# A hand-timed scan schedule: every slot constant moved, and one state merge out of four dropped

## The reference

```
L0: gated linear recurrence, y = Wout(silu(ga) * gb * scan(f, z)) + x
    top-1 of 4 experts, silu(x Wg) * (x Wu), Wd
L1: xz = W_in x ; xc = silu(conv4(x) + b) ; dt, B, C = W_x xc
    delta = softplus(W_dt dt + b_dt) ; A = -exp(A_log)
    state[n] = exp(delta * A[n]) * state[n] + (delta * xc) * B[n]     n = 0..15
    y = sum_n state[n] * C[n] + D * xc ; y = y * silu(z) ; out = W_out y + b_out
    out = out * silu(bw x) + x                (binarised weight)
```

## Time and profile before

| | |
|---|---|
| median of 3 runs | 1398.58 us (1398.46 to 1400.58) |
| the profiled execution | 1398.58 us, span of its instructions 1396.8 us |
| granted TensorE clock, mean | 0.997 |
| state-space part, first scan to last | 605.7 to 1379.3 us |
| a chunk in its middle, scan to scan | 97.5 us |
| accumulating DMAs that merge states | 31, of 1026 KB each |

### The profile page before, as it was taken

The page is one execution under the profiler, slowest core; times in us unless marked ns, Lnnn a source line. Parts: engine busy times, 40 slices in busy tenths (PEclk is TensorE's granted clock), DMA queues, the critical chain, the costliest instruction groups (busy, mean ns, idle before and its releaser), DMA issues.

```text
span 1396.8 us, 23943 instructions
## 1 busy us (share of the span) xinstructions
PE 1331.7 (95%) x8796; PEld 1064.4 (76%) x8796; DVE 1008.4 (72%) x1358; ACT 875.5 (63%) x1459; POOL 854.0 (61%) x482
## 2 busy tenths in 40 slices
PE   7999999999999999989899999999999999998998
PEld 4444559999999988967667877777778678677777
DVE  7755543323322343578998999999999989989897
ACT  3211121111111132559999999999999999999983
POOL 3222211222222222348989989989989899899894
PEclk9999999999999999999999999999999999999999
DMA  9931126677667755415453553735636554634542
GB/s 298 397 112 60 53 74 232 246 260 266 251 245 254 276 204 211 162 49 90 110 103 79 99 116 77 138 92 97 133 66 125 107 99 93 136 78 104 124 102 65
DMA packets 113187, 205.46 MB, mean 147 GB/s; under 512 B 57647, under 2 KB 84399, under 8 KB 108214
## 3 DMA queue, kind: packets, MB, share of 16 engines
q1 hardware_dynamic: 93814, 146.75, 31.9%
q0 software_dynamic: 19264, 57.26, 19.8%
HBM read 141.78 MB, written 31.00 MB: 124 GB/s over the span
## 4 chain that ended last, share of the span: by engine, by line
PE 54%; ACT 31%; DVE 9%; issue 3%; POOL 2%; DMA 1%; SPq 0%; DVEq 0%; ACTq 0%; POOLq 0%
PE bank L1666 18%; ACT dA L947 13%; ACT dbuT L936 10%; PE bank L1611 9%; PE bank L1679 9%; DVE hst L1509 4%; PE bank L1840 4%; PE bank L1720 2%; PE bank L1848 2%; PE bank L1712 2%; PE bank L1731 2%; PE bank L1860 2%; PE bank L1641 2%; ACT xpad L878 1%; ACT xpad L874 1%
## 5 line engine op out<-in xcount | busy, mean ns | idle before, releaser
L1509 DVE TENSOR_TENSOR_SCAN hst<-dA,carry,bank 128x512 f32<-128x512 f32 x512 | 628.8, 1267 | 37.3 <-PE bank L1840 29.9
L740 POOL TENSOR_TENSOR hst<-hst,c_bc 128x2048 f32<-128x2048 f32 x127 | 550.1, 4425 | 42.1 <-DVE hst L1509 31.3
L947 ACT ACTIVATE dA<-delta,negA 128x512 f32<-128x512 f32 x512 | 354.5, 713 | 1.0 <-DVE hst L1509 0.9
L1840 PE MATMUL bank<-ident,dbuT 128*128 128x128 f32 x2048 | 310.8, 276 | 27.4 <-DVE hst L1509 23.6
L1840 PEld LDWEIGHTS bank<-ident,dbuT 128*128 128x128 f32 x2048 | 239.5, 141 | 127.2 <-DVE hst L1509 57.1
L936 ACT ACTIVATE dbuT<-duT,bT 128x512 f32<-128x512 f32 x382 | 271.6, 712 | 0.3 <-PE bank L1840 0.3
L1666 PEld LDWEIGHTS bank<-f_sb,w_gu 128*128 128x128 f32 x2240 | 256.0, 192 | 4.7 <-issue 2.1
L1666 PE MATMUL bank<-f_sb,w_gu 128*128 128x128 f32 x2240 | 256.9, 275 | 0.7 <-ACT f_sb L804 0.7
L1860 PE MATMUL bank<-ident,hst 128*128 128x128 f32 x1520 | 209.7, 273 | 1.8 <-DMA hst<-hst 1.7
L670 POOL TENSOR_TENSOR x_sb<-x_sb,neg_half 128x1 f32<-128x1 f32 x35 | 22.7, 648 | 271.3 <-DVE x_sb L1290 271.3
L1860 PEld LDWEIGHTS bank<-ident,hst 128*128 128x128 f32 x1520 | 174.2, 141 | 2.6 <-DMA hst<-hst 2.6
(11 more groups left out here) (220 smaller groups left out, 1663.9 us busy)
## 6 DMA issues: line engine op xcount, KB each, us to landing
w_gu<-in_w_gu SPq DMA_DIRECT2D x35, 2048.0 KB
c_bc<-c_rows SPq DMA_DIRECT2D x64, 512.0 KB, 4.4
hst<-hst POOLq DMA_DIRECT2D x31, 1026.0 KB, 9.1
sorted_x<-sg_a SPq DMA_DIRECT2D x12, 387.0 KB, 11.7
x_sb<-sorted_x SPq DMA_DIRECT2D x35, 129.0 KB
x_sb<-in_x SPq DMA_DIRECT2D x8, 512.0 KB, 7.8
w_d<-in_w_d SPq DMA_DIRECT2D x1, 4096.0 KB, 19.9
x_mix<-x_sb SPq DMA_DIRECT2D x1, 4096.0 KB, 30.6
```

What stands on the lines that cost most here:

```text
L740: pool.tensor_tensor(h[:, :, :CH], h[:, :, 1:], c, ALU.mult).then_inc(hc_ready, 1)
L947: act.activation(dA[:, at % DA_BUFS, :], delta[q % B][:, d, :], ACT.Exp, scale=negA[:, d, n:n + 1]).then_inc(dA_ready, 1)
L1509: v.tensor_tensor_scan(h[:, d, 1:], dA[:, at % DA_BUFS, :], bank[4 + u % 2][:], carry1[q % B][:, n, d:d + 1], ALU.mult, ALU.add).then_inc( ...
L1840: ins = pe.transpose(bank[4 + u % 2][:, i * P:(i + 1) * P], dbuT[(DS * q + n) % DBU_BUFS][:, i, d * P:(d + 1) * P], ident[:])
```

## The change

It only replaces tables. Nearly every placement moves by one to six units. Besides that the pair `5: 4` leaves `MERGES` and `LAST_MERGES`: states 4 and 5 are now both added by TensorE, and since (4, d) has no entry in `SUM_AT` it falls to slots 31 to 34. POOL makes states 5, 6, 8 and 11 of dbuT instead of 4, 6, 7 and 9. `DL0` moves to bank A and `XN0` to bank B, so that all four `DL` products share bank A. The tables of the last chunk (`LAST_...`) stay, but it uses `SUM_AT`, `PE_Z`, `PE_G`, `PE_SKIP` and the new merges too.

```diff
-POOL_SPREADS = (4, 6, 7, 9)
+POOL_SPREADS = (5, 6, 8, 11)
-PE_X = (-3, -1, 2, 3, 4, 5, 8, 9)
-PE_G = (11, 12, 15, 16)
-PE_DT = (21, 24, 25, 27)
-PE_DL = (29, 32, 37, 44)
-PE_BC = 31
-PE_BT = 47
-PE_DUT = (49, 51, 52, 56)
-PE_Z = (9, 9, 10, 11, 11, 12, 14, 14)
-PE_XN = (53, 55)
-PE_YF = (21, 30, 34, 36)
-PE_OUT = (40, 42, 43, 45, 46, 47, 49, 51)
-PE_SKIP = (17, 18, 18, 18)
-ACT_X = (1, 5, 10, 11)
+PE_X = (-4, -1, 0, 3, 5, 8, 9, 10)
+PE_G = (12, 14, 15, 16)
+PE_DT = (22, 23, 24, 26)
+PE_DL = (28, 34, 36, 41)
+PE_BC = 32
+PE_BT = 48
+PE_DUT = (51, 53, 54, 55)
+PE_Z = (9, 10, 10, 11, 11, 12, 13, 14)
+PE_XN = (55, 57)
+PE_YF = (21, 32, 35, 37)
+PE_OUT = (39, 40, 42, 44, 46, 47, 49, 51)
+PE_SKIP = (17, 18, 19, 19)
+ACT_X = (3, 6, 11, 16)
-ACT_SOFT = (35, 39, 41, 47)
-ACT_DUT = (51, 54, 55, 59)
-ACT_YF = (24, 36, 39, 40)
-DVE_CONV = (1, 3, 4, 5, 6, 7, 9, 10, 11, 12, 13, 14)
-DVE_GATE = (8, 9, 10, 12)
+ACT_SOFT = (34, 38, 43, 44)
+ACT_DUT = (54, 55, 57, 59)
+ACT_YF = (29, 37, 38, 40)
+DVE_CONV = (2, 3, 4, 5, 6, 8, 9, 10, 11, 12, 13, 14)
+DVE_GATE = (8, 9, 10, 11)
 DVE_DT = 28
-DVE_DELTA = (31, 36, 43, 47)
-DVE_BC = 32
-DVE_BT = 48
+DVE_DELTA = (31, 36, 41, 47)
+DVE_BC = 35
+DVE_BT = 50
-DVE_RESULT = (46, 52)
-DVE_XN = (54, 57)
-POOL_DU = (7, 9, 11, 12)
+DVE_RESULT = (45, 54)
+DVE_XN = (57, 59)
+POOL_DU = (6, 9, 9, 10)
-MERGES = {1: 0, 5: 4, 9: 8, 13: 12}
-LAST_MERGES = {1: 0, 5: 4, 9: 8}
+MERGES = {1: 0, 9: 8, 13: 12}
+LAST_MERGES = {1: 0, 9: 8}
...
-          (15, 1): 6, (15, 2): 8, (15, 3): 3, ... (5, 0): 38, (5, 1): 38, (5, 2): 35,
-          (5, 3): 41, (6, 0): 34, (6, 1): 35, (6, 2): 39, (6, 3): 35, (7, 0): 42, (7, 1): 46, (7, 2): 43, (7, 3): 48,
+          (15, 1): 8, (15, 2): 7, (15, 3): 7, ... (5, 0): 36, (5, 1): 40, (5, 2): 35,
+          (5, 3): 40, (6, 0): 42, (6, 1): 40, (6, 2): 43, (6, 3): 42, (7, 0): 44, (7, 1): 46, (7, 2): 45, (7, 3): 48,
...
-BANK_OF = {..., "DL0": 1, "DL1": 0, "DL2": 0, "DL3": 0, ... "XN0": 0, "XN1": 1, ...}
+BANK_OF = {..., "DL0": 0, "DL1": 0, "DL2": 0, "DL3": 0, ... "XN0": 1, "XN1": 1, ...}
```

More of the change, by code:

```diff
@@ L89 @@
 ACT_BC = None
-DVE_RESULT = (46, 52)
-DVE_XN = (54, 57)
-POOL_DU = (7, 9, 11, 12)
+DVE_RESULT = (45, 54)
+DVE_XN = (57, 59)
+POOL_DU = (6, 9, 9, 10)
 POOL_RES = 13
-MERGES = {1: 0, 5: 4, 9: 8, 13: 12}
-LAST_MERGES = {1: 0, 5: 4, 9: 8}
-SUM_AT = {(13, 0): 6, (13, 1): 4, (13, 2): 8, (13, 3): 6, (14, 0): 2, (14, 1): 2, (14, 2): 1, (14, 3): 2, (15, 0): 4,
[5 rows of a table removed]
-BANK_OF = {"X0": 0, "X1": 1, "X2": 0, "X3": 1, "G0": 0, "G1": 1, "DT": 0, "DL0": 1, "DL1": 0, "DL2": 0, "DL3": 0,
-           "BT": 0, "DUT0": 0, "DUT1": 0, "DUT2": 1, "DUT3": 0, "XN0": 0, "XN1": 1, "YF0": 1, "YF1": 0, "YF2": 1,
+MERGES = {1: 0, 9: 8, 13: 12}
+LAST_MERGES = {1: 0, 9: 8}
+SUM_AT = {(13, 0): 4, (13, 1): 4, (13, 2): 6, (13, 3): 6, (14, 0): 4, (14, 1): 3, (14, 2): 3, (14, 3): 5, (15, 0): 4,
[5 rows of a table added]
+BANK_OF = {"X0": 0, "X1": 1, "X2": 0, "X3": 1, "G0": 0, "G1": 1, "DT": 0, "DL0": 0, "DL1": 0, "DL2": 0, "DL3": 0,
+           "BT": 0, "DUT0": 0, "DUT1": 0, "DUT2": 1, "DUT3": 0, "XN0": 1, "XN1": 1, "YF0": 1, "YF1": 0, "YF2": 1,
            "YF3": 1, "BC": 1, "OUT0": 1, "OUT1": 1}
```

## The result

The changed kernel takes 1421.51 us (median of 4 runs, 1421.28 to 1421.61), beside 1399.43 us for the kernel before in the same sittings (4 runs, 1398.46 to 1400.58): a ratio of 1.0157, 95% interval 1.014 to 1.0175. It is slower, as forecast, by 22 us (1.6%) where 11 were forecast, and lies above the range of 1390 to 1418.

A forecast was written before the change was run, and what follows sets the result against it. No engine stood out; the chain ran DVE, TensorE to the skip term, then ACT, with TensorE to take ACT's place. Six middle chunks x 1.9 = 11.4, less 0.5 for chunk 0, on 1398.58 gave 1409 us, range 1390 to 1418.

The forecast's parts named there:

- ACT's stretch: From the skip term on, ACT nearly alone on the chain for 54 us; to get 2.45 us shorter per chunk.
- xc at t = 35.95: ACT's step after the skip term: predicted to start at t = 36.0, 0.7 us later in the chunk.
- no wait of BC: BC, now in the other bank, no longer waits for `DL0`: a stall of 1.71 us of TensorE gone.
- `DL0` and `DL2` wait 0.30 and 0.81: Slots 28 and 36: `DL0` waits 0.4 us for DVE's copy of dt, `DL2` 0.8 for `make_delta` 1.
- the idle in front of slot 39: Slots 37 and 38 are light and TensorE can't run ahead of the scans: 0.7 us idle.
- 22.65 - 21.8: TensorE's time from slot 8 to the skip term's end: 22.65 us to slot 19, before 21.8 to slot 18.
- the walk: Slot-by-slot estimate of a middle chunk from single-chunk prices, reaching scan 23 at 40.7 us and scan 48 at 77.9.
- the chunk is 77.9 + 21.5 = 99.4: +1.9 us: Middle chunk: scan 48 at 77.9 us, then 21.5 to the next chunk's first scan; 1.9 us longer than before.
- Chunk 0 ... ACT's saving counts: -0.5: Chunk 0: TensorE has room without output projection, so ACT's saving counts; -0.5 us, between -1.7 and +0.7.
- ACT sets the pace: Rival, chance 0.20: TensorE's light slots absorb the additions, each of 7 chunks gains 1.75 us; 1386 us.
- A wash: Rival, chance 0.12: BC's removed wait pays for the four additions, ACT's saving for the later skip term; 1398.6 us.
- More bank waits: Rival, chance 0.10: ACT's lead is too small and `DL3` in slot 41 waits 1.8 us per chunk; 1422 us.

The follow-up runs named there:

- The `DL` run: Kernel after with `DL0` and `DL2` claimed one slot later, PE_DL = (29, 34, 37, 41): 1412.94 us.
- POOL's tables alone: Kernel before with only POOL_SPREADS and POOL_DU as changed: 1402.90 us.
- the run with slots 40 to 44 spread out: Kernel after with two additions of state 5 moved from slot 40, to slots 38 and 39: 1421.22 us.
- the kernel with three mendings: Kernel after with two `DL` claims one slot later, two additions moved out of slot 40 and the merge of state 4 put back: 1409.73 us.
- mid: Kernel before with only the tables of slots 21 to 47 as changed, merge of state 4 kept: 1431.23 us.
- the BC edit with POOL's tables: Kernel before with the BC edit and the change's POOL_SPREADS and POOL_DU: 1405.35 us.
- the BC edit: Kernel before with B and C's product two slots later, DVE_BC at 35 and two turned y one slot later: 1409.72 us.
- the skip-term run: The kernel with three mendings, with the skip term back in its old slots (17, 18, 18, 18): 1416.83 us.
- ACT's copy moved: Kernel before with the BC edit and ACT's copy of the second turned y in slot 34 instead of 36: 1418.11 us.

## Why the prediction was half right

**Right.** The direction and its reason: TensorE's work and its bank waits take the place of ACT's stretch. By its own signs: xc at t = 35.95; an idle before it below 1 us; no wait of BC; `DL0` and `DL2` wait 0.30 and 0.81 (0.4 and 0.8 were written), and the idle in front of slot 39 is 0.59 (0.7 was written); DVE's longest idle behind scan 23 before scan 44, ended by L1840 (over the whole chunk the 0.94 before scan 21 and the 1.80 before scan 23 are longer, which was not written); TensorE on the chain behind xc, though only to t = 70.

Part of the hit at xc is luck: 22.65 - 21.8 and the 0.25 in slot 9 make 1.1, not 0.7, and the 0.7 came of setting the walk's 35.8 against the measured 35.1, where the same walk gives 34.7 for the kernel before.

The rule of the Trainium skill to rotate banks ("Perfetto Trace Analysis", Matmuls) agrees with the trace in one place, not two: `DL2` waits 0.81 us for its bank, while `DL0`'s 0.30, which the prediction counted to the rule, is for its operand. The `DL` run shows what such waits cost, by claiming later; no run puts one of these products into the other bank by itself. The rule on the same page of the Trainium skill to look for the engine with the highest occupancy, and to judge TensorE by its weight loads ("Identifying the Most-Contended Engine"), misleads here: these fill 74.0 of 96 us, yet 1.74 us more of TensorE's work cost 1.05 us. Whether less work for ACT, the busiest by that rule, would pay, no run shows.

**Failed: the term "the chunk is 77.9 + 21.5 = 99.4: +1.9 us".** It measured 100.75, +3.2. No long wait was overlooked; the walk drifted:

| stretch | predicted | after | missed by |
|---|---|---|---|
| to scan 23 | 40.7 | 40.6 | -0.1 |
| 23 to 31 | 11.0 | 11.2 | +0.2 |
| 31 to 37 | 9.1 | 9.5 | +0.4 |
| 37 to 44 | 11.2 | 11.6 | +0.4 |
| 44 to 48 | 5.9 | 5.95 | +0.05 |
| 48 to the next chunk | 21.5 | 21.8 | +0.3 |

The prices were those of groups that run on, 0.44 for four transposes. Behind a wait a group takes longer to the next start: 0.47 at 1076.90 in TensorE's rows above, 0.97 for the `DL2` product that was priced 0.86. A slot of TensorE that waits for a scan starts 1.43 us after that scan's start (1075.47 to 1076.90, 1063.08 to 1064.51), where 1.32 was priced. The walk also left out the idle of 0.59 before 1064.51, behind `DL0`. In the tail it had 0.7 us above DVE's 20.8 for small waits, and 1.0 was measured, with a stall of 0.51 us before scan 57. That these small prices add up to 1.35 is read from the walk, not tested one by one, so the cause of this excess stays open in part.

**Failed: "Chunk 0 ... ACT's saving counts: -0.5".** It was +1.4, give or take the 1.4 that the clock makes there. The saving counts in no chunk of the old schedule: with POOL's tables alone chunk 0 went from 100.29 to 100.39, with the low clock in the same place of the chunk. In the new one it only prevents a wait: chunk 0 is 104.2 without them, beside 103.0 in the run with slots 40 to 44 spread out, whose clock is low in nearly the same place.

**Not in the sum: the 600 us ahead of the first scan.** 2.8 us of the profiled execution arose in code that the diff doesn't touch (next but one section). No reading of the tables could have given them.

Of the 11.6 us between 1409.5 and the profiled 1421.1, the middle chunks are 6.6, chunk 0 1.9, the first layer 2.8, the end 0.3. The upper end of my range for a middle chunk was +2.7, since only the unknown bank waits went into it, not the drift of a walk through 64 slots.

**The rivals.** "ACT sets the pace", with its gain of 1.75 us a chunk, fell by POOL's tables alone. "A wash" needed the two `DL` waits to vanish, and they stand; in the kernel before, BC's wait could not have been turned into a gain either, because it covered another wait. "More bank waits" gave nearly the measured time (1422) for another reason than the real one, which is luck; its wait exists (1.31 us) but only without POOL's tables.

What stays open: of the 1.75 us that the kernel with three mendings still loses, 0.66 lie before scan 23 and 1.22 between 23 and 48, and the second part was not taken apart.

## What to carry to other kernels

A schedule in which four engines are over nine tenths busy is a set of ties. The engine on the chain is then only the one that came last: move or cut its work alone and see whether anything moves before counting on it. A long wait may cover a second one behind it in the same bank or buffer; before counting it as a gain, look up when the next claim behind it could have started. When a walk through many slots gives the sum, take the prices behind waits as well as those of running groups, and widen the range by what they add up to; and parts of a schedule that were fitted together can't be valued one by one, for here they sum to three times the whole.

## What the runs showed of the hardware

**The granted clock in the first layer differs between executions in code that the diff doesn't touch.** A window of 4 us, before and after (columns as in the earlier trace rows; the clock is the last but two):

```profile
62.00:66.00 4.00, 3.14 (x27) 2.67 (x28) 2.88 (x10) 0.69 (x1) 0.81 (x1) 1.00 1.08 430
```

```profile
62.00:66.00 4.00, 3.24 (x14) 2.05 (x15) 2.10 (x9) 0.69 (x1) 0.91 (x1) 0.50 1.06 412
```

Before it is 1.00, which is 2.4 GHz; after it is 0.50, the lower level of 1.2, and the twelve matmuls of L1641 take 2.76 us there, before 1.47. In both, TensorE had just waited 3.2 us for DVE. The first scan comes at 605.5 to 605.8 us in five traces (before, mid, the `DL` claims, all three mendings, the BC edit with POOL's tables), at 606.7 to 607.5 in ten, at 608.5 to 608.7 in three (after, the BC edit, the skip-term run). The granted clock at 62 to 70 us sorts them: 1.00 in the five, 0.79 in nine of the ten, 0.57 to 0.58 in the three. The tenth (606.7, ACT's copy moved) has 1.00 too and loses its time at 77 us, where DVE waits 4.38 instead of 3.06 for a DMA. The groups follow no table, and what makes the clock fall in one execution and not in another was not found. The kernel before itself took from 1396.99 to 1400.92 us over all sittings of the study. So a difference of 1.4 or even 2.8 us between single executions says nothing about the schedule. Of the 22.5 us between the two profiled executions 2.8 are of this kind. For the medians it isn't known: the other four executions of the kernel after have no trace, and they took 1421.28 to 1421.61 us at a mean granted clock of 0.998, beside 1421.13 at 0.996.

**The clock falls behind some waits of TensorE and not behind others of the same length.** In the BC edit with POOL's tables `DL1` waits 1.47 to 1.48 us in each chunk. In most of them the clock stays at 1.00; in chunk 4 it falls behind the wait. The windows of chunk 4, then the stalled product and the group behind it:

```profile
1050.00:1054.00 4.00, 2.39 (x20) 1.92 (x18) 3.52 (x4) 3.94 (x7) 4.00 (x2) 1.00 1.07 200
1054.00:1058.00 4.00, 3.75 (x18) 2.35 (x22) 2.71 (x3) 4.00 (x8) 4.00 (x2) 0.57 0.56 91
1058.00:1062.00 4.00, 4.00 (x61) 3.80 (x54) 2.71 (x4) 1.81 (x3) 3.47 (x5) 1.00 0.00 0
```

```profile
1054.25 1.79 PE L1767 MATMUL bank<-x_ld,w_dt 128*128 128x512 f32 x2 [1.48 <-ACT conv_y L865]
1055.83 1.06 PE L1840 MATMUL bank<-ident,dbuT 128*128 128x128 f32 x4
```

The product takes 1.79 us instead of 1.12 and the group behind it 1.06 instead of 0.60. Scans 34 and 35 wait 1.29 us each, and the chunk is 99.85 us instead of 98.2. It is so again in chunk 6 (0.57 in the window, 99.5 us), in chunk 1 of the BC edit alone (0.60, 100.5 us instead of 98.8), and in chunks 2, 4 and 6 of the kernel with ACT's copy moved (0.64 to 0.71, 101.55 instead of 100.1). In chunks 1 to 6 of the kernel after the clock is 1.00 in the like windows. (In this last kernel TensorE waits 2.94 us for a scan in chunk 4, and as long in chunk 5, where the clock stays.) So behind a wait of TensorE of 1.5 us or more a chunk can lose another 1.3 to 1.7 us to the clock. That the wait is what lets the clock fall is suggested by the order in time, not tested.
